# Attention scores in split precision: three products per head on 64 partitions each instead of two on 128, written for two heads at a time, with eight probability buffers

## The reference, cut to what matters

```python
latent_kv = x @ w_kv_down                      # x: 8 batches, 1024 tokens, 256 channels
k, v = split(latent_kv @ w_kv_up)              # 16 heads of 64
q = x @ w_q
att = jnp.einsum('bqhd,bkhd->bhqk', q, k) * scale
att = softmax(where(causal, att, -inf))
y = jnp.einsum('bhqk,bkhd->bqhd', att, v)
x = layernorm(x + y @ w_out)
x = layernorm(x + mixture_of_experts(x))       # 8 experts, top tokens of each
```

## Time and profile before

| what | value |
| --- | --- |
| time, median of 3 runs | 3080.33 us (3075.99 to 3082.09) |
| the profiled execution | 3079.45 us, its span 3077.6 us |
| attention | 0 to about 2020 us of the span |
| one pair of heads | 30.23 us |
| busy share of the span: PE, DVE, ACT, POOL | 97%, 68%, 62%, 50% |

### The profile page before, as it was taken

How to read it: one execution, slowest core, us unless ns; L and a number is a source line. 1 busy time by engine, 2 the same in 40 slices (tenths; PEclk the granted TensorE clock), 3 DMA queues, 4 the chain that set the end, 5 groups by cost and what they waited for, 6 DMA issues and landing times. The chain is left out here.

```text
span 3077.6 us, 62761 instructions
## 1 busy us (share of the span) xinstructions
PE 2989.0 (97%) x19264; PEld 2393.8 (78%) x19264; DVE 2078.5 (68%) x5938; ACT 1910.1 (62%) x4173; POOL 1539.3 (50%) x1623
## 2 busy tenths in 40 slices
PE   8999999999999999999999999999989999999996
PEld 6776767777776776776767677689989999999996
DVE  6777777777777777777767767745968865545446
ACT  6676777777677767676767767645534444444443
POOL 4444444444444444444444434446757776666665
PEclk9999999999999999999999999999989999999998
DMA  7776877787777777777778687677634444434425
GB/s 183 202 205 184 205 207 192 200 212 186 204 207 191 196 204 196 194 201 212 185 203 210 188 204 200 166 245 268 237 122 118 107 102 107 106 79 90 112 50 164
DMA packets 394705, 542.01 MB, mean 176 GB/s; under 512 B 78696, under 2 KB 293480, under 8 KB 394368
## 3 DMA queue, kind: packets, MB, share of 16 engines
q1 hardware_dynamic: 352320, 487.43, 58.0%
q0 software_dynamic: 25152, 33.75, 6.6%
q10 hardware_dynamic: 16896, 16.78, 1.5%
HBM read 211.85 MB, written 158.16 MB: 120 GB/s over the span
## 5 line engine op out<-in xcount | busy, mean ns | idle before, releaser
L288 POOL TENSOR_SCALAR prob<-prob,inv 128x128 f32<-128x128 f32 (+7 forms) x1024 | 766.6, 752 | 1130.3 <-DVE inv L760 1129.9
L755 DVE CUSTOM_DVE_ANT_0 s_ps<-s_ps,mask 128x128 f32<-128x128 f32 (+7 forms) x1024 | 774.0, 756 | 444.3 <-PE s_ps L455 438.1
L644 ACT ACTIVATE prob<-s_ps,neg_max 128x128 f32<-128x128 f32 (+7 forms) x1024 | 760.2, 743 | 214.5 <-DVE neg_max L755 206.2
L470 PE MATMUL t_ps<-ident,prob 128*128 128x128 f32 x3328 | 525.6, 274 | 20.1 <-POOL prob L288 13.7
L470 PEld LDWEIGHTS t_ps<-ident,prob 128*128 128x128 f32 x3328 | 393.4, 140 | 69.8 <-POOL prob L288 17.5
L737 ACT ACTIVATE prob_t<-t_ps 128x512 f32<-128x512 f32 x512 | 305.8, 597 | 207.4 <-PE t_ps L470 207.1
L1821 PE MATMUL e_y<-w_hi,hid_hi 128*128 128x256 f32 (+1 forms) x1088 | 312.0, 287 | 0.0
L1822 PE MATMUL e_y<-w_lo,hid_hi 128*128 128x256 f32 (+1 forms) x1088 | 308.0, 283 | 0.0
L1823 PE MATMUL e_y<-w_hi,hid_lo 128*128 128x256 f32 (+1 forms) x1088 | 308.0, 283 | 0.0
L1682 POOL DMA_INDIRECT acc_d<-yg,idx_all x128 | 211.3, 1651 | 189.9 <-ACT yg L1895 161.1
L454 PE MATMUL s_ps<-w_lo,w_hi 128*128 128x512 f32 (+3 forms) x768 | 291.6, 382 | 7.4 <-ACT prob L644 7.4
(11 more groups left out here) (264 smaller groups left out, 6736.3 us busy)
## 6 DMA issues: line engine op xcount, KB each, us to landing
k_hh<-k_high SPq DMA_DIRECT2D x128, 256.0 KB, 4.5
y_d<-c_res SPq DMA_DIRECT2D x128, 256.0 KB, 4.3
k_lz<-k_low SPq DMA_DIRECT2D x126, 256.0 KB, 5.4
s_d<-squares SPq DMA_DIRECT2D x63, 512.0 KB, 2.9
late_t<-s_d SPq DMA_DIRECT2D x252, 128.0 KB, 3.4
w_lo<-k_high SPq DMA_DIRECT2D x124, 256.0 KB, 4.5
c_yt<-y_d SPq DMA_DIRECT2D x60, 512.0 KB, 7.0
s_d<-squares SPq DMA_DIRECT2D x63, 384.0 KB, 2.6
```

The source lines that it names most:

```text
L288: pool.tensor_scalar(pr, pr, inv[:, s % 4:s % 4 + 1], 1.0, ALU.mult, ALU.mult).then_inc(norm_done, 1)
L470: mm = pe.transpose(t_ps[s % 2][:, to * P:(to + 1) * P], prob[s % 4][:, j * P:(j + 1) * P], ident[:])
L644: act.activation(prob[s % 4][:, 0:(q + 1) * P], score_part(s), ACT.Exp, scale=-1.0, bias=neg_max[:, s % 4:s % 4 + 1], accum_out=total[:, s ...
L755: dve.tensor_tensor_reduce(part, part, mask[:, T - (q + 1) * P:T], 1.0, -MASKED, ALU.add, ALU.min, neg_max[:, s % 4:s % 4 + 1]).then_inc(m ...
```

## The change

Score matmuls take their operands where ACT and DVE write them: `q_high`, `q_low`, `k_high`, `k_low` now exist twice (u), with head h on partitions 64h to 64h + 63, and nothing is copied. For each tile q and chunk of keys there are six matmuls of 64 partitions: high x high, high x low, low x high, each for head 0 and then head 1, the heads into different PSUM buffers. Both heads of a q are thus written as one group, and the group waits for the exponentials of both heads of the q before. The ten placing DMAs a pair, `q_hl`, `k_hh`, `k_lz` and the waits on them are gone. `prob`, `neg_max`, `total` and `inv` have eight buffers instead of four, and the lists of slots are new.

```diff
+    PB = 8
-        q_high, q_low, k_high, k_low = (sb(n, [P, T], F32R) for n in ("q_high", "q_low", "k_high", "k_low"))
+        q_high, q_low = ([R.q_hl[i], sb(f"q_of_1{i}", [P, T], F32R)] for i in range(2))
+        k_high, k_low = ([R.k_hh[i], sb(f"k_of_1{i}", [P, T], F32R)] for i in range(2))
-        prob = [sb(f"prob{i}", [P, T]) for i in range(4)]
+        prob = [sb(f"prob{i}", [P, T]) for i in range(PB)]
...
-        SCORES_AT = [[4], [5], [6], [7], []] + [[s + 3] for s in range(5, 13)] + [[16], [17, 18], [19]]
+        SCORES_AT = {0: 2, 1: 3, 5: 4, 7: 5, 9: 6, 11: 7, 13: 8, 14: 9}
-        MAXIMA_AT = [[4], [5], [6], [7], []] + [[s + 3] for s in range(5, 13)] + [[16], [17], []]
+        MAXIMA_AT = {0: [4, 5], 1: [6, 7], 5: [8, 9], 7: [10, 11], 9: [12, 13], 11: [14, 15], 13: [16, 17], 14: [18, 19]}
...
-            for u in range(2):
-                for h in range(2):
-                    pool.memset(k_lz[u][h][:].bitcast(F32), 0.0).then_inc(const_ready, 1)
...
-                if keys:
-                    place_queries(n + 2, u)
-                if keys:
-                    place_keys(n + 2, u)
...
-                for c in range(g + 1):
-                    w = slice(c * HALF, min((c + 1) * HALF, width))
-                    out = score_part(s)[:, w]
-
-                    pe.matmul(out, q_hl[u][h][:, cols], k_hh[u][h][:, w], start=True, stop=False)
-                    mm = pe.matmul(out, q_hl[u][h][:, cols], k_lz[u][h][:, w], start=False, stop=True)
-                mm.then_inc(scores_done, 1)
+                for c in range(q // 4 + 1):
+                    w = slice(c * HALF, min((c + 1) * HALF, (q + 1) * P))
+                    for i, (a, b) in enumerate(((q_high, k_high), (q_high, k_low), (q_low, k_high))):
+                        for h in range(2):
+                            rows = slice(64 * h, 64 * h + 64)
+                            mm = pe.matmul(score_part(2 * q + h)[:, w], a[u][rows, cols], b[u][rows, w],
+                                           start=(i == 0), stop=(i == 2))
+                            if c == q // 4 and i == 2:
+                                mm.then_inc(scores_done, 1)
...
-                            pe.wait_ge(exp_done, 16 * n + (t - 3 if t < 8 else t - 1))
-                            scores(n, u, t)
+                    q = SCORES_AT.get(s, 0)
+                    if 2 <= q < 8:
+                        pe.wait_ge(exp_done, 16 * n + (2 * q - 2 if q < 4 else 2 * q))
+                        scores(n, u, q)
+                    elif q and after:
+                        pe.wait_ge(low_done, 4 * n + 8)
+                        pe.wait_ge(exp_done, 16 * n + 16)
+                        scores(n + 1, 1 - u, q - 8)
...
-                if 16 * n + s >= 4:
-                    act.wait_ge(turned, 16 * n + s - 3)
+                if 16 * n + s >= PB:
+                    act.wait_ge(turned, 16 * n + s - PB + 1)
```

More of the change, by code:

```diff
@@ L225, in x_piece @@
             return i // 2, halves(i % 2)
[L227 to L236, removed]
         def latents(n, m, s):
@@ L328, in store_y @@
                              y[g][:]).then_inc(y_out[g], 16)
[L330 to L342, removed]
             def write_squares(n, w):
@@ L358, in read_squares, with turn @@
                                  ).then_inc(late_in, 16)
[L360 to L372, removed]
+            def turn(b, m, u, weights=True, reload=True, squares=True):
                 n = NPAIR * b + m
@@ L440, in _ @@
                         sp.dma_start(part, y_d[0][:, 2 * c:2 * c + 2, :]).then_inc(R.yt_in, 16)
-                turn(B - 1, m, m % 2, weights=m + 3 < NPAIR, keys=m + 2 < NPAIR, reload=False,
+                turn(B - 1, m, m % 2, weights=m + 3 < NPAIR, reload=False,
                      squares=m + 1 < NPAIR)
@@ L606, in slots @@
                 for s in range(8 * g, 8 * g + 8):
-                    for t in SCORES_AT[s]:
-                        if t < 16:
-                            if first and t == 8:
-                                keys_ready(0)
-                            pe.wait_ge(exp_done, 16 * n + (t - 3 if t < 8 else t - 1))
-                            scores(n, u, t)
-                        elif after:
-                            if t == 16:
-                                keys_ready(n + 1)
-                            pe.wait_ge(exp_done, 16 * n + (15 if t % 2 == 0 else 16))
-                            scores(n + 1, 1 - u, t - 16)
+                    q = SCORES_AT.get(s, 0)
[6 more added lines that the diff above has]
+                        scores(n + 1, 1 - u, q - 8)
                     turn(n, s)
@@ L708, in first @@
                 high(1, 1, 0)
-                exp(0, 0)
-                exp(0, 1)
+                for s in range(4):
+                    exp(0, s)
             def slots(n, m, g, after):
@@ L715, in slots @@
                     _, q, h = step(s)
-                    for t in EXPS_AT[s]:
+                    for t in EXPS_AT.get(s, []):
                         if t < 16 or after:
@@ L739, in slots @@
                     for t in LATE_EXPS_AT.get(s, []):
-                        exp(n, t)
+                        if t < 16 or after:
+                            exp(n, t)
                     if s - 1 in Q_AT and after >= 2:
@@ L838, in slots @@
                     for t in EARLY_INVERSES_AT.get(s, []):
-                        invert(n, t)
-                    for t in MAXIMA_AT[s]:
+                        if t < 16 or after:
+                            invert(n, t)
+                    for t in MAXIMA_AT.get(s, []):
                         if t < 16 or after:
                             maximum(n, t)
-                    for t in INVERSES_AT[s]:
+                    for t in INVERSES_AT.get(s, []):
                         if t < 16 or after:
@@ L854, in slots @@
                         copy_late(n, s)
-                    for t in LATE_MAXIMA_AT.get(s, []):
-                        if after:
-                            maximum(n, t)
                     if (m, s) in X_SPLIT and not last_batch(n):
```

93 lines of the change are left out of this document (36 added, 57 removed).

## The result

The changed kernel takes 3320.62 us (median of 4 runs, 3316.86 to 3323.36) against 3079.01 for the kernel before (4 runs, 3075.99 to 3082.09): a ratio of 1.0784 [1.0765, 1.0803], 242 us slower. The forecast was 3321.

The account below looks back on a forecast made before the run. PE was taken to set the pace. A pair: -2.2 + 2.1 + 4.6 - 0.5 = +4.0 us, over 63 pairs +252; with -10 for the DMAs, 3079.45 + 242 = 3321 us, range 3250 to 3420.

Parts of the forecast that it names:

- The wait that is added: Ahead of score groups PE waits for both heads' exponentials: stalls of 1.3, 1.7 and 1.6 us, +4.6 a pair.
- Products and changes of form: Score products side by side on row halves gain 2.2 us a pair; 15 added tiling-mode switches cost 2.1.
- What vanishes: Half of PE's present short waits for four kinds of results goes away: -0.5 us a pair.
- the pair: Time for one pair of heads in attention: about 34.2 us, from 30.23 before.
- Placing DMAs: Dropping ten hidden copies a pair may shorten DVE's wait for the squares' transfers: -10 us in all, 0 to -30.
- Eight buffers: Free ACT from waiting for a turn of four heads ago; by themselves they bring nothing.
- Loads bare: Rival: a half's weight load can't run while that half multiplies, 4 us a pair, 3570 us; chance 0.03.
- no overlap: Rival: products on the two row halves run one after the other, 3705 us; chance 0.08.
- covered chain: Rival: PE's work between groups covers the two maxima, -0.6 us a pair, 3031 us; chance 0.05.
- Dearer halves: Rival: row halves overlap, but weight loads go in turn or a mode switch costs 0.28 us: 3400 to 3420; chance 0.15.

Follow-up runs that it names:

- e1: Kernel before with the change's slot lists, eight buffers and both heads as one group, old 128-partition products, placing DMAs left out: 3328.81 us, ratio 1.0807.
- e6: Changed kernel with head 1's maximum and exponential cut to 128 columns for q of 4 and more: 3179.22 us, ratio 1.0323.
- e7: Changed kernel with nothing left out, value products spread to slots between the groups that stall: 3182.54 us, ratio 1.0333.
- e5: Changed kernel with only head 1's maximum cut to 128 columns for q of 4 and more: 3304.05 us, ratio 1.0725.
- e10: Changed kernel without the third score product (low queries x high keys): 3251.88 us, ratio 1.0540.
- e3: Changed kernel with head 0's three products of a chunk issued first, then head 1's three: 3322.50 us, ratio 1.0786.
- e2: Kernel before without its placing DMAs, operands placed for pair 0 only and reused: 3059.86 us, ratio 0.9932.
- e9: Kernel before without placing DMAs and with eight probability buffers instead of four, slots unchanged: 3059.41 us, ratio 0.9925.
- e8: Changed kernel with all products of head 0 of a group written ahead of all of head 1's: 3374.66 us, ratio 1.0959.

## Why the prediction was right, point by point

**The wait that is added** (+4.6 a pair): right in mechanism, place and size. Stalls of 1.23, 1.66 and 1.63 us stand where 1.3, 1.7 and 1.6 were forecast, and none at q = 5 to 6; 275 us in all against some 290. e1 (grouping alone), e6 (chain cut) and e7 (work beside it) each move it as the mechanism asks. The chain's length was right, its description incomplete: not DVE's two maxima alone are serial, ACT's two exponentials are too, and equally long (e5).

**Products and changes of form** (-2.2 + 2.1): the sum was right, 34.29 to 34.16 us from e1 to after, and e10 gives the price of a pass. That the halves run side by side, loads too, is seen. Without a stall ahead a change of form was mis-sized: 0.35 us a score group (entering 0.095 and a first step 0.105 longer, leaving about 0.10 and 0.05) where 0.28 stood. Behind a stall nothing is added on entering: there the first step is 0.335 to 0.337 in e1 too, which changes no form, and the 0.095 lies inside the stall. Fifteen halves of 0.35 less three times 0.2 are 2.0 a pair, so the 2.1 of the sum held. The reason given for the overlap in the expectation of e3, that the heads are issued in turn, was wrong.

**What vanishes** (-0.5) and **the pair** (34.2): 34.16 measured; from 30.25 that is +3.9 instead of +4.0. That something vanishes fits e1: its stalls of the same three places are 1.24, 1.64 and 1.57, 4.4 together, and against e2 its pair grew by 4.05, so some 0.4 went.

**Placing DMAs** (-10, from 0 to -30): the row named was the right one, the size is -20 (e2). **Eight buffers**: nothing (e9).

**A term was missing.** The first pair stalls too, ahead of the stretch in which the 63 pairs were counted. After, and before, up to the first value products of group 0:

```profile
41.43 1.51 PE L393 MATMUL s_ps<-w_lo,w_hi 64*128 64x512 f32 x12 [1.30 <-ACT prob L574]
...
46.49 1.65 PE L393 MATMUL s_ps<-w_lo,w_hi 64*128 64x512 f32 x12 [1.63 <-ACT prob L574]
...
52.19 0.55 PE L393 MATMUL s_ps<-k_of,q_of 64*128 64x128 f32 x6 [1.62 <-ACT prob L574]
...
53.25 1.08 PE L436 MATMUL o_ps<-tri,v 128*64 128x512 f32 x4
```

```profile
46.14 1.08 PE L496 MATMUL o_ps<-tri,v 128*64 128x512 f32 x4
```

In the first pair no value products of a pair before fill the slots, so the group of q = 6 (at 41.43) waits too. That is +7 us; the 63 steps from there to the last pair (53.3 to 2247.9 after, 46.1 to 2006.4 before) bring +234, with the placing's gain in them. 234 + 7 = 241, and the sum had 252 - 10 = 242. Its parts were off by more than its total: 63 x 3.91 = 246 instead of 252, -20 instead of -10, and +7 missing. Missing too are eight stretches of attention at the lower clock (0.99 on average against 1.00 in the earlier trace rows), which made the value products of group 0 some 14 us longer in all than 2.37 us each, and 2.5 us more behind the last pair: the spans of the two traces differ by 244.0. That all this cancels to 1 us is luck.

**Rivals.** Loads bare, no overlap and a covered chain are excluded by the steps by twos and the stalls. Dearer halves hold in part: 0.07 us a group where no stall stands ahead.

No version that does all the work beat the kernel before; e2 is faster only by what it leaves out. Whether the new products pay in a kernel with a third and a fourth PSUM buffer of scores, which would free the group, wasn't tried. Nor was a wait for each head: with head 0's products ahead and behind head 0's exponential alone, they could start some 1.05 us earlier (the exponentials start at 671.89 and 672.94), an estimate that leaves out what the order of e8 costs.

## What to carry to other kernels

Before you join two buffers' work into one group, work out the chain that empties both, and set it against what the waiting engine has between two groups: here the difference was paid every time, whatever the group itself saved. Average slack of the other engines (DVE and ACT at 70% here) doesn't help. Where the chain can't be cut, moving independent work between the groups is worth more (138 us here) than shortening the second head's work on one of two engines that are equally long (17 us).

## What the runs showed of the hardware

- PE takes matmuls on an idle row half ahead of older ones that wait for the other half: over two of them at once (10 ns after the first, e3); with five waiting, only when 0.59 us later three were left (e8). The Trainium skill (TensorE: Matmul & The Clock Gate, The mechanism) says that matmuls start and end in program order and only weight loads are taken ahead; e3 and e8 disagree.
- Two matmuls of 64 partitions and 512 columns on the two row halves start 3 to 4 ns apart and take one step of 0.23 us, with their loads (0.18 us each) inside (the group at 674.09 of after).
- A change to row halves and back costs 0.35 us around a block (the group at 669.02 of after).
- In most pairs of e10 two stops of PE of 1.6 us were followed by a stretch at a granted clock of 0.50, in which sixteen value products took 4.06 us instead of 2.37; in after, with the same stops, there are 8 such stretches.
